# Scan stage: layernorm statistics by ScalarE passes with accumulated sums, and every eighth first state weighted by VectorE

## The reference

```python
def _layernorm(x, axis=-1, eps=1e-05):
    m = jnp.mean(x, axis=axis, keepdims=True)
    v = jnp.var(x, axis=axis, keepdims=True)
    return (x - m) / jnp.sqrt(v + eps)
# the scan, D_STATE = 16 states for each of the 512 channels
dt_raw, b_ssm, c_ssm = parts of einsum('bld,kd->blk', x, W_x)
dt = softplus(einsum('blr,dr->bld', dt_raw, W_dt) + b_dt)
d_a = exp(dt[..., None] * -exp(A_log)); dbx = dt[..., None] * b_ssm * x[..., None]
h = da_t * h + dbx_t;  y = einsum('bdn,bn->bd', h, c_t)     # over 512 tokens
return y + x * D_param
# the mixture of experts, after its own layernorm
out = sum over the top 6 of 64 experts (SwiGLU, 352 wide) + silu(x @ sw_gate) * (x @ sw_up) @ sw_down
```

## Time and profile before

| stretch | what runs | DVE busy | POOL busy | PE busy | ACT busy |
|---|---|---|---|---|---|
| whole span | | 53% | 46% | 85% | 38% |
| 46 to 1169 us | 256 scan steps | 981.3 us | 974.6 us | 902.5 us | 636.1 us |
| 1286 to 1765 us | experts of the first mixture | 99.7 us | 89.2 us | 379.2 us | 52.5 us |

### The profile page before, as it was taken

How to read it: one execution, slowest core, us unless ns; L and a number is a source line. 1 busy time by engine, 2 the same in 40 slices (tenths; PEclk the granted TensorE clock), 3 DMA queues, 4 the chain that set the end, 5 groups by cost and what they waited for, 6 DMA issues and landing times.

```text
span 3363.0 us, 38115 instructions
## 1 busy us (share of the span) xinstructions
PE 2864.7 (85%) x13772; PEld 1530.6 (46%) x13772; DVE 1784.8 (53%) x3707; ACT 1281.1 (38%) x2678; POOL 1541.3 (46%) x955
## 2 busy tenths in 40 slices
PE   4578878888887967888857999999889899999998
PEld 2455544544554533333324555555444444444443
DVE  5888988888889822122115666665423333322221
ACT  4555656455564511111114666667512111011110
POOL 5998888888879701222104555554300000121212
PEclk7688989899898978999978999999989999999999
DMA  4354453535434447999960000000044221799997
GB/s 179 126 177 143 148 180 116 191 123 174 165 125 161 141 155 252 349 340 345 342 207 1 26 26 26 26 14 14 26 160 153 91 76 33 252 349 330 349 348 195
DMA packets 198957, 557.67 MB, mean 166 GB/s; under 512 B 24944, under 2 KB 26864, under 8 KB 198256
## 3 DMA queue, kind: packets, MB, share of 16 engines
q1 hardware_dynamic: 181072, 514.19, 44.1%
q0 software_dynamic: 16640, 39.86, 5.2%
q10 hardware_dynamic: 1056, 1.18, 0.1%
HBM read 480.42 MB, written 74.74 MB: 165 GB/s over the span
## 4 chain that ended last, share of the span: by engine, by line
PE 51%; DVE 12%; POOL 10%; SPq 8%; ACT 7%; DMA 7%; issue 4%; POOLq 0%; DVEq 0%; ACTq 0%
PE bank L923 8%; PE bank L911 6%; PE bank L890 6%; PE bank L984 6%; POOL arena L1659 4%; PE bank L1031 4%; SPq L1894 3%; SPq L1883 3%; PE bank L1088 3%; DVE arena L1165 3%; PE bank L1065 3%; POOL arena L1665 3%; PE bank L1010 2%; DVE bank L1165 2%; DMA out<-arena 2%
## 5 line engine op out<-in xcount | busy, mean ns | idle before, releaser
L1659 POOL TENSOR_TENSOR arena<-arena 128x1024 f32<-128x1024 f32 x256 | 611.4, 2389 | 57.3 <-PE bank L862 44.0
L862 PE MATMUL bank<-arena 128*128 128x128 f32 x2048 | 316.4, 307 | 194.2 <-POOL arena L1665 194.2
L1518 ACT ACTIVATE bank<-arena 128x512 f32<-128x512 f32 x512 | 343.0, 688 | 317.5 <-DVE arena L1165 201.4
L1748 POOL TENSOR_TENSOR arena<-arena 128x2048 f32<-128x2048 f32 (+3 forms) x128 | 296.6, 2320 | 279.6 <-DVE arena L1386 279.6
L862 PEld LDWEIGHTS bank<-arena 128*128 128x128 f32 x2048 | 264.9, 158 | 283.5 <-POOL arena L1665 226.8
L923 PE MATMUL bank<-arena 128*128 128x512 f32 (+1 forms) x768 | 372.8, 630 | 15.8 <-DVE arena L1188 15.8
L1581 ACT ACTIVATE arena<-arena 128x256 f32<-128x256 f32 (+3 forms) x512 | 286.0, 562 | 200.4 <-DVE arena L1377 170.0
L1665 POOL TENSOR_TENSOR arena<-arena 128x512 f32<-128x512 f32 x256 | 326.1, 1274 | 77.3 <-DVE arena L1165 77.1
L1165 DVE TENSOR_TENSOR_SCAN arena<-bank,arena 128x512 f32<-128x512 f32 x256 | 310.8, 1214 | 71.9 <-ACT bank L1518 69.3
L984 PE MATMUL bank<-arena 128*64 128x352 f32 x2048 | 333.6, 481 | 0.0
L1165 DVE TENSOR_TENSOR_SCAN bank<-bank,arena 128x512 f32<-128x512 f32 x256 | 308.5, 1205 | 0.0
(11 more groups left out here) (136 smaller groups left out, 4210.1 us busy)
## 6 DMA issues: line engine op xcount, KB each, us to landing
arena<-scratch_bc SPq DMA_DIRECT2D x128, 1024.0 KB, 5.4
arena<-in_w_gate SPq DMA_DIRECT2D x128, 704.0 KB, 12.4
arena<-in_w_up SPq DMA_DIRECT2D x128, 704.0 KB, 14.2
arena<-in_w_down SPq DMA_DIRECT2D x128, 512.0 KB, 15.2
arena<-in_w_down SPq DMA_DIRECT2D x128, 192.0 KB, 17.2
scratch_x<-arena SPq DMA_DIRECT2D x16, 1024.0 KB, 4.3
scratch_xn<-arena SPq DMA_DIRECT2D x15, 1024.0 KB, 8.6
arena<-scratch_x SPq DMA_DIRECT2D x48, 256.0 KB, 5.7
```

Of the source, the lines that this page charges most:

```text
L862: i = nc.tensor.matmul(y[:, t * P:(t + 1) * P], w[:, n, t * P:(t + 1) * P], p.ident, is_transpose=True, start=False, stop=g == GROUPS - 1 ...
L1518: nc.scalar.activation(bank[p.da_bank(k, n)][:, :], block_of(p.dt, b, c), ACT.Exp, scale=p.alog[:, c, state:state + 1]).then_inc(*p.decaye ...
L1659: nc.gpsimd.tensor_tensor(out=p.hb[k % HB], in0=over(block_of(p.dtx, b, c), 1, NG), in1=p.bc[k // 2 % NBC][:, 0], op=ALU.mult).then_inc(*p ...
L1748: nc.gpsimd.tensor_tensor(out=own, in0=own, in1=over(p.rden[:, k % 2, :], 2, width), op=ALU.mult).then_inc(*p.divided.up(k))
```

## The change

The S and F norms of the scan stage no longer use BN_STATS on VectorE. ScalarE reads x twice: `total` is four Identity passes whose accumulated sums are the row sums (their elementwise output goes to s_xn and is overwritten later), then the sums times -1/H give the shift; `square` is four Square passes with that shift as bias, whose accumulated sums are the squared deviations. GpSimd's `rstd` scales by 1/H and adds eps in one instruction. `total` takes over the waits of `apply` for s_xn, that of `stats` for the loaded x or for `x1`. The plan changes with it: an F norm has one step more, `prepare_steps` one more and begins at step 9 of a batch instead of 8. And in every step with k % 8 == 0 VectorE weights the first state too (SBUF times SBUF, the form of GpSimd's L1665), and GpSimd does not.

```diff
+LENT = 8
...
 def front_steps(m, q):
     f = ("F", m, q)
-    yield [("stats", f)]
-    yield [("rstd", f)]
     if m == 0:
+        yield [("total", f)]
+        yield [("square", f)]
+        yield [("rstd", f)]
         yield []
+    else:
+        yield [("stats", f)]
+        yield [("rstd", f)]
     yield [("apply", f), ("xn_out", m, q)]
...
 def prepare_steps(b):
     s = ("S", b)
-    yield [("stats", s), ("rstd", s)]
+    yield [("total", s)]
+    yield [("square", s), ("rstd", s)]
     yield []
...
-            if k % STEPS == 8 and b + 1 < BATCH:
+            if k % STEPS == 9 and b + 1 < BATCH:
                 coming = prepare_steps(b + 1)
...
-        for n, by in enumerate(("pool", "dve")):
+        for n, by in enumerate(("pool" if k % LENT else "dve", "dve")):
             PE.wait_ge(p.weighted[by], k)
...
         V.wait_ge(p.bc_in[k // 2 % NBC], k // 2)
+        if k % LENT == 0:
+            V.wait_ge(p.scanned, k, 0)
+            nc.vector.tensor_tensor(out=h[:, 0, :], in0=h[:, 0, :], in1=p.bc[k // 2 % NBC][:, 1, 0, :], op=ALU.mult)
         V.wait_ge(p.scanned, k, NG - 1)
...
+    def total(n):
+        x, xn, (_, mv, _, shift) = p.norm(n)
         before = p.norm_before(n)
         if before is not None:
             A.wait_ge(p.ring_of(before).made, "turn", before, HC - 1)
             if before[0] == "F":
                 A.wait_ge(p.xn_out, before[1], before[2])
+        if n[0] == "S":
+            A.wait_ge(p.x_in[n[1] % 2], n[1])
+        else:
+            A.wait_ge(p.x1_added, n[2], HC - 1)
+        for t in range(QT):
+            i = nc.scalar.activation(xn[:, t, :], x[:, t, :], ACT.Identity, accum_out=mv[:, t, 0:1])
+        i.then_inc(*p.totalled.up(n))
+        A.wait_ge(p.totalled, n)
+        nc.scalar.mul(shift, mv[:, :, 0], -1.0 / H).then_inc(*p.centred.up(n))
+
+    def square(n):
+        x, xn, (_, mv, _, shift) = p.norm(n)
+        A.wait_ge(p.centred, n)
+        for t in range(QT):
+            i = nc.scalar.activation(xn[:, t, :], x[:, t, :], ACT.Square, bias=shift[:, t:t + 1],
+                                     accum_out=mv[:, t, 1:2])
+        i.then_inc(*p.squared.up(n))
...
     def rstd(n):
         _, _, (_, mv, out, shift) = p.norm(n)
-        G.wait_ge(p.varied, n)
         if p.applier(n) == "act":
-            nc.gpsimd.tensor_scalar(shift, mv[:, :, 0], -1.0, None, ALU.mult)
-        nc.gpsimd.tensor_scalar(out, mv[:, :, 1], EPS, None, ALU.add).then_inc(*p.lifted.up(n))
+            G.wait_ge(p.squared, n)
+            nc.gpsimd.tensor_scalar(out, mv[:, :, 1], 1.0 / H, EPS, ALU.mult, ALU.add).then_inc(*p.lifted.up(n))
...
     def weigh_c(k):
+        if k % LENT == 0:
+            return
         h = p.hb[k % HB][:, 0, :]
```

More of the change, by code:

```diff
@@ L673, in semaphores @@
         self.varied = sig("varied", "stats")
+        self.totalled, self.centred = sig("totalled", "total"), sig("centred", "total")
+        self.squared = sig("squared", "square")
         self.lifted = sig("var_lifted", "rstd")
@@ L689, in semaphores @@
         self.fed = sig("fed", "feed")
-        self.weighted = {"pool": sig("weighted_pool", "weigh_c"), "dve": sig("weighted_dve", "scan")}
+        self.weighted = {"pool": sig("weighted_pool", "weigh_c", where=lambda k: k % LENT),
+                         "dve": sig("weighted_dve", "scan")}
         self.y_summed = sig("y_summed", "sum")
@@ L1113, in stats @@
         x, _, (st, mv, _, _) = p.norm(n)
-        if n[0] == "S":
-            V.wait_ge(p.x_in[n[1] % 2], n[1])
-        elif n[0] == "A":
+        if n[0] == "A":
             V.wait_ge(p.xa_in[n[1] % NXA], n[1])
-        elif n[1] == 0:
-            V.wait_ge(p.x1_added, n[2], HC - 1)
         else:
@@ L1425, in barrier @@
         A.wait_ge(p.stage_done, i, 4)
-    def apply(n):
-        if p.applier(n) != "act":
-            return
-        x, xn, (_, _, rstd, shift) = p.norm(n)
+    def total(n):
+        x, xn, (_, mv, _, shift) = p.norm(n)
         before = p.norm_before(n)
@@ L1435, in apply @@
                 A.wait_ge(p.xn_out, before[1], before[2])
+        if n[0] == "S":
[14 more added lines that the diff above has]
+        i.then_inc(*p.squared.up(n))
+    def apply(n):
+        if p.applier(n) != "act":
+            return
+        x, xn, (_, _, rstd, shift) = p.norm(n)
         A.wait_ge(p.rstd_made, n)
@@ L1603, in weighed @@
             *ring.taken_by["act"].up("weigh", n))
-    work = {"constants": constants, "barrier": barrier, "apply": apply, "xn_out": xn_out,
+    work = {"constants": constants, "barrier": barrier, "total": total, "square": square,
+            "apply": apply, "xn_out": xn_out,
             "route1": route1, "turned": turned, "bc_out": bc_out, "dtr_out": dtr_out,
@@ L1634, in rstd @@
         _, _, (_, mv, out, shift) = p.norm(n)
-        G.wait_ge(p.varied, n)
         if p.applier(n) == "act":
-            nc.gpsimd.tensor_scalar(shift, mv[:, :, 0], -1.0, None, ALU.mult)
-        nc.gpsimd.tensor_scalar(out, mv[:, :, 1], EPS, None, ALU.add).then_inc(*p.lifted.up(n))
+            G.wait_ge(p.squared, n)
+            nc.gpsimd.tensor_scalar(out, mv[:, :, 1], 1.0 / H, EPS, ALU.mult, ALU.add).then_inc(*p.lifted.up(n))
+        else:
+            G.wait_ge(p.varied, n)
+            nc.gpsimd.tensor_scalar(out, mv[:, :, 1], EPS, None, ALU.add).then_inc(*p.lifted.up(n))
         G.wait_ge(p.lifted, n)
```

## The result

The changed kernel takes 3376.19 us (median of 11 runs, 3369.27 to 3386.02), the kernel before 3363.65 us: a ratio of 1.0048, interval [1.0033, 1.0063]. It is slower by 12.5 us by the medians and by 16 by the ratio, where 3363 and no change were forecast. The profiled execution took 3385.21 us, its span is 3383.4 us. It lies 9 us above the median. What stands behind `merge` takes 2087 to 2103 us in the thirteen profiled executions of this document, with no order that fits the edits, so the traces are read up to `merge` and what a kernel is worth is read from the medians.

The account below looks back on a forecast made before the run. GpSimd was taken to pace part of each batch at 3.54 us a step, then TensorE. Terms 3 - 2.8 - 15.4 + 1.2 - 1.8 + 3 + 6 + 6 = -0.8 gave 3363 us, no change (chance 0.36), range 3342 to 3388.

Parts of the forecast that it names:

- the lent weightings: 32 scan steps: each costs VectorE 1.8 us (0.6 to 4.3) and gains GpSimd 0.6 (0 to 1.22).
- +3 at the picks: Batches 2, 4 and 6, lent step 16 among the picks, VectorE as full as TensorE: +1 us each, bounds 0 and 8.
- Start, +3: The first norm stands on the path and takes 6.1 us in place of 2.8; bounds +1 and +3.5.
- F norm, -2.2 each: Batches 1 to 7: GpSimd's 2.50 us idle mostly goes, its weighting and `rstd` shrink; seven times, -15.4 us in all.
- S norm +0.8: Batches 1 to 6: `rstd` waits about 1 us on GpSimd for `square`; +0.8 us each, bounds -0.3 and +3.5.
- The wait for the loaded x: S norm, batches 1 to 6: ScalarE reaches `total` before x has landed and waits 1 to 2.5 us.
- Dense TensorE, +6: Batches 1 to 7: the shared expert's moved pieces put TensorE 93 us over GpSimd's pace, before 87; bounds 0 and 12.
- Tail, +6: After the scan: `fetch` 5.5 us earlier, three `sd` (17.7) behind its landing, later work 5.8 faster; bounds +2 and +12.
- GpSimd sets the pace everywhere: Rival, whole scan: GpSimd's saved work counts in every part, 3333 us, or half of it, 3348; chance 0.34.
- ScalarE's passes hold up the exps: Rival, scan norms: each F norm +1.4, each S norm +2.5 us; 3400 us, or half of it, 3382; chance 0.20.
- The scan ends as before: Rival: TensorE's dense part takes back GpSimd's gain; start, dense part and tail remain, +15 us, 3380; chance 0.10.
- The prediction's sign that `weigh_c` would wait less: Scan, GpSimd: if the forecast is right, `weigh_c` waits less in total than 77 us in the profile after.

Follow-up runs that it names:

- e2: The changed kernel without the lent weightings, so ScalarE's passes and the new plan alone: ratio 1.0013 to the kernel before.
- e10: The changed kernel without the lent weightings and with the 20 weight DMAs moved behind the last `fetch` of batch 6's shared expert: ratio 0.9929.
- e5: The changed kernel, but in every eighth step nobody weights the first state (32 of 512 products left out): ratio 0.9992.
- e6: The changed kernel, but in lent steps the first recurrence writes its PSUM bank and VectorE weights from there, with one SBUF input only: ratio 1.0035.
- e1: The kernel before with the lent weightings alone, norms and plan as before: ratio 1.0072.
- e3: The kernel before with every piece placed as in the changed plan, old statistics on VectorE, an empty piece for `square`, no lending: ratio 1.0047.
- e4: The changed kernel without lending and in the old cadence, `square` and `rstd` in one step, `prepare_steps` from step 8: ratio 1.0041.
- e9: The changed kernel with 32 lent weightings in steps 10, 12, 20 and 26 of each batch instead of 0, 8, 16 and 24: ratio 1.0018.

## Why the prediction was wrong, step by step

**The failed step is the lent weightings.** The prediction has them as a gain: -2.5 of batch 0, 0.6 at each of seven F norms and six steps 8, -1.8 in batch 7, +3 at the picks, together about -9. With and without them (changed against e2) the scan ends 12.1 us later in the traces (8.8 against e10, whose scan is e2's), and the ratio is 0.0035 higher, 12 us: an error of 21 us. The rest of the sum was off by 4 the other way: without lending's share it gives +8.3, and e2 measured +4. The two make the 17 us between the forecast's -0.8 and the measured 16.

The price of one was right: 1.8 taken, 1.74 measured. What failed is the sentence "I take 1.8; GpSimd gains 0.6" as a saving, and behind it the reading of who sets the pace. The prediction put GpSimd's 3.54 us a step over part of each batch, over all of batch 0, and gave VectorE 0.54 of room there. Of the 255 distances between recurrences of the kernel before, 100 are under 3.1 us: these are VectorE's own pace, 2.98 and 3.05. Another 29 are 3.57 to 3.65, which looks like GpSimd's 3.54 and is not: VectorE does one instruction of 0.6 us more in them and idles 0.1 us at most. At GpSimd's pace, 3.51 to 3.55 with VectorE idle for 0.5, are 7. After a stall GpSimd is ahead by what `feed` may run ahead, and VectorE is the one that catches up. There GpSimd's 1.22 us saved are worth nothing (e5), and each microsecond on VectorE delays what follows.

In all eight steps 8 of e2 the next recurrence stands 3.05 us behind. In the changed kernel it comes later than that by the lent weighting's own time less 0.28 us: 5.40 behind one of 5.68, 1.40 behind 1.68, 0.70 behind 0.98, 2.18 behind 2.46. These delays are 14.5 us in the eight, of which 9.4 are left by step 12. In e6, without the lock, it is 0.38 at each of the eight. At steps 24 of batches 1 and 6, where e2's distance is 6.4 and 6.0, nothing is lost. Here is one of the steps 8 in rows. In e5 (same norms and plan, nobody weights) batch 6's step 8, VectorE (L1170 recurrence, L1222 the router's first reduction), then ScalarE (L1573 the router's exp behind that reduction):

```profile
920.53 1.21 DVE L1170 TENSOR_TENSOR_SCAN arena<-bank,arena 128x512 f32<-128x512 f32 x1
...
923.58 1.21 DVE L1170 TENSOR_TENSOR_SCAN arena<-bank,arena 128x512 f32<-128x512 f32 x1
...
929.77 0.41 DVE L1222 TENSOR_REDUCE arena<-arena 128x4 f32<-128x256 f32 x1
```

```profile
930.61 0.35 ACT L1573 ACTIVATE arena<-arena 128x64 f32<-128x64 f32 x1 [0.54 <-DVE arena L1225]
```

And in the changed kernel (L1175 lent weighting, L1225 the reduction, L1576 the router's exp):

```profile
927.66 1.21 DVE L1170 TENSOR_TENSOR_SCAN arena<-bank,arena 128x512 f32<-128x512 f32 x1
...
929.91 2.46 DVE L1175 TENSOR_TENSOR arena<-arena 128x512 f32<-128x512 f32 x1
...
932.89 1.21 DVE L1170 TENSOR_TENSOR_SCAN arena<-bank,arena 128x512 f32<-128x512 f32 x1
...
939.26 0.41 DVE L1225 TENSOR_REDUCE arena<-arena 128x4 f32<-128x256 f32 x1
...
942.02 1.23 DVE L1170 TENSOR_TENSOR_SCAN arena<-bank,arena 128x512 f32<-128x512 f32 x1 [2.15 <-ACT bank L1548]
```

```profile
939.91 0.35 ACT L1576 ACTIVATE arena<-arena 128x64 f32<-128x64 f32 x1 [2.24 <-DVE arena L1228]
...
941.26 2.72 ACT L1548 ACTIVATE bank<-arena 128x512 f32<-128x512 f32 x4
```

In e5 the next recurrence stands 3.05 us behind that of step 8, here 5.2 (927.66 to 932.89). The 2.2 us go on: reduction, router's exp, which ScalarE waits for with the scan's exps queued behind it, and the recurrence after. The rise of VectorE's waits for exps from 69.3 to 104.7 us is not lending's: they are 63.8 with lending alone (e1), 95.5 with the plan alone (e3) and 118.4 with passes and plan (e2).

**Start, +3:** the first recurrence starts 4.9 to 5.2 us later than before in six kernels with the passes and 2.4 and 2.7 in two (the changed one is at 2.7); in the four others with the old statistics it is 0.1 to 2.4. The means differ by 3.4: right, though single executions pass the bound of 3.5.

**F norm, -2.2 each, bounds -2.8 and +1.4; S norm +0.8:** right in sign as a sum, wrong in its places. Without lending's share, start, seven F and six S norms make -3.7 in it; e2 ends its scan 9.1 us before e3, whose pieces stand alike, and e10 5.9 before. But the F norms do not bring this. In steps 0 to 9 of batches 1 to 7 e2 falls 8.8 us behind e3 (e10: 8.1), and it gains 22.7 in steps 9 to 32 of the eight batches, 14.0 of them in steps 9 to 16, where the S norm is, which the prediction had as a loss. Batch 2's F norm, `x1` and the next recurrence on VectorE, in e2:

```profile
324.07 0.68 DVE L1183 TENSOR_TENSOR arena<-arena,bank 128x512 f32<-128x512 f32 x1
328.26 1.22 DVE L1170 TENSOR_TENSOR_SCAN arena<-bank,arena 128x512 f32<-128x512 f32 x1 [3.51 <-ACT bank L1548]
```

And in e3 (L1127 the old statistics):

```profile
325.68 0.68 DVE L1179 TENSOR_TENSOR arena<-arena,bank 128x512 f32<-128x512 f32 x1
326.39 2.47 DVE L1127 BATCH_NORM_STATS2 arena<-arena 128x6 f32<-128x512 f32 x4
...
329.20 1.19 DVE L1169 TENSOR_TENSOR_SCAN arena<-bank,arena 128x512 f32<-128x512 f32 x1
```

VectorE waits 3.51 us for the exp behind `total` where the statistics took 2.8. With the step behind `square` its two steps take 11.2 us in e2 and 9.5 in e3; the prediction's 4.6 and 4.3 from `x1` on were near (4.2 and 4.0). GpSimd's wait did go away as the term had it: in front of `weigh_c` behind the F norm at about 612 us it is 0.23 us in e2, against 2.45 in e4 and 2.50 in the earlier trace rows. But that wait was not what set the time. e4, then e2:

```profile
619.74 1.27 POOL L1696 TENSOR_TENSOR arena<-arena 128x512 f32<-128x512 f32 x1 [2.45 <-DVE arena L1168]
```

```profile
613.07 1.26 POOL L1698 TENSOR_TENSOR arena<-arena 128x512 f32<-128x512 f32 x1 [0.23 <-DVE arena L1170]
```

In e4 an `sd` stands beside `x1` in batches 2 to 7 as before, and each of these F norms costs 1.2 us at once, near the upper bound of 1.4. In batches 2 to 6 most of it is back by step 9. The 10 us that e4 loses behind its start of 4.9 are not seven equal losses: steps 0 to 16 lose 3.1 us in batch 1, 1.8 in batch 4 and 4.2 in batch 7, and 0.2 to 0.5 in each of the other four. Why there stays open.

The wait for the loaded x (1 to 2.5 us) did not come: `total` waited 41.3 us for `x1` and for no load.

**Dense TensorE, +6:** e3's scan ends 6.2 later. The number is right; that the loss lies beside the projections is not shown, for over the scan e3 is at times 8 us behind the kernel before and at times 8 ahead of it.

**Tail, +6, from 5.5 earlier and 12 more behind the landing:** the landing (1199.34 and 13.85 later) came 2.1 us behind that of before while the last recurrence was 9.1 late, so 7.0 sooner behind it; from landing to the last `su`'s end it is 54.2 us against 42.0. +5.2 in all: right, and four other kernels with the new plan and the weights first have 5.1 to 6.1 (e3, e5, e6, e9). e2 has 11.2: its 54.2 is 58.8, since the clock came back later (its router took 4.91 us, 3.76 here, and its last two `sd` 13.13, 10.94 here).

```profile
1199.34 13.85 DMA arena<-scratch_x
...
1214.02 7.35 PE bank L932 x12
...
1223.31 3.76 PE bank L885 x32
1227.06 10.94 PE bank L932 x24
...
1263.94 3.45 PE bank L920 x8
```

**The rivals.** "GpSimd sets the pace everywhere" is refuted by e5. "ScalarE's passes hold up the exps" names a wait that is there at each F norm and in e4's time, but with the new plan the passes do not make the loss (e2). Its 3382 is near the measured time for another reason. "The scan ends as before", 3380, is near it too, and its scan did not end as before. The prediction's sign that `weigh_c` would wait less in total than 77 us failed, at 109.5, and it pointed at the right part: the wait is 76 to 84 us in the kernels that do not lend (e2 76.2, e3 77.4, e4 84.0), 96.3 in e5 and 135.7 in e1. The case that happened, VectorE's pace and the lent microseconds added to it, was not among the rivals.

## What to carry to other kernels

Before taking work from one engine to another, read the distances between repeated instructions, not the busy shares: a distance near an engine's own cycle time names the engine that may set the pace there, and that engine's idle time in it confirms or refutes it (3.65 us here was VectorE with one instruction more, not GpSimd's 3.54). Change one part at a time: here two parts cost 14 to 16 us alone and 4 together, and the third hid the result. And look at what small transfer stands behind a block of large ones in a queue: one `fetch` behind 20 weight DMAs was worth 41 us, three times the whole change.

## What the runs showed of the hardware

A VectorE instruction with both inputs in SBUF did not always get the next turn when GpSimd's instruction ended: it missed up to three hand-overs (7.62 us for one of 0.67). With one input in PSUM the same product took 0.67 to 0.675 in all 32 places. The Trainium skill says the same of the second form (SBUF — State Buffer, Who interferes with whom: at most one SBUF input does not contend); that the waiting engine can lose several turns in a row is what these runs show. And a pass of ScalarE with an accumulated sum is two instructions, 0.62 or 0.71 us and 0.19 for reading the sum out; four come to 2.6 (Identity) and 2.9 (Square), the latter the 2.9 that attention's rows gave.
